# Keys and values of an 8-head attention made in an earlier stage, kept in DRAM and fetched batch by batch

## The reference

```python
x = x + tanh(g_xattn[0]) * cosine_similarity(layernorm(x), c)       # L0 attention
x = x + tanh(g_ffn[0])   * top2_of_8_linear_experts(layernorm(x))   # L0 ffn
x = x + tanh(g_xattn[1]) * film_s4d_block(layernorm(x), c)          # L1: top-32 attention, FiLM, S4D
x = x + tanh(g_ffn[1])   * adapter_of_least_loss(layernorm(x))      # L1 ffn
x = x + tanh(g_xattn[2]) * attention_16_heads(layernorm(x), c)      # L2 attention
x = x + tanh(g_ffn[2])   * fp8_linear(layernorm(x))                 # L2 ffn
x = x + tanh(g_xattn[3]) * attention_8_heads(layernorm(x), c)       # L3 attention
x = x + tanh(g_ffn[3])   * top2_of_8_gelu_experts(layernorm(x))     # L3 ffn
```

```python
q = (x @ Wq).reshape(B, Nq, 8, 64)
k = (context @ Wk).reshape(B, 128, 8, 64)
v = (context @ Wv).reshape(B, 128, 8, 64)
attn = softmax(einsum('bihd,bjhd->bhij', q, k) * SCALE)
out = einsum('bhij,bjhd->bihd', attn, v).reshape(B, Nq, 512) @ Wo + bo
```

## Time and profile before

| | |
|---|---|
| device time, median of 3 runs | 1424.72 us (1424.49 to 1426.15) |
| the profiled execution | 1425.62 us, its span 1423.8 us |
| mean granted TensorE clock | 0.868 |
| busy share of the span | PE 83%, DVE 70%, ACT 48%, POOL 39% |
| top-32 attention with its start and end | from about 211 to 479.6 us |
| convolution | 479.6 to about 494 us |
| 8-head attention with the fp8 layer | from about 895 to 1155 us; its first scores start at 921.7 us |

### The profile page before, as it was taken

How to read it: one execution, slowest core, us unless ns; L and a number is a source line. 1 busy time by engine, 2 the same in 40 slices (tenths; PEclk the granted TensorE clock), 3 DMA queues, 4 the chain that set the end, 5 groups by cost and what they waited for, 6 DMA issues and landing times. The chain is left out here.

```text
span 1423.8 us, 30767 instructions
## 1 busy us (share of the span) xinstructions
PE 1177.9 (83%) x10551; PEld 807.0 (57%) x10551; DVE 995.2 (70%) x3895; ACT 689.7 (48%) x2022; POOL 548.2 (39%) x770
## 2 busy tenths in 40 slices
PE   4768664767766858996899998699999989999998
PEld 3534322434444535663777777266667667776776
DVE  6767568999999269976577877677776644444433
ACT  3344245677775244432345454366666643333343
POOL 4576665677764246534122321334433310000000
PEclk8788785776675779998799999699999999898989
DMA  6400104000001311101000000000000000000000
GB/s 171 99 0 1 46 12 131 16 24 27 27 23 45 115 64 42 38 23 34 3 3 3 3 4 3 1 1 1 1 2 1 2 0 1 15 0 15 0 16 15
DMA packets 61249, 36.62 MB, mean 26 GB/s; under 512 B 19477, under 2 KB 58992, under 8 KB 61106
## 3 DMA queue, kind: packets, MB, share of 16 engines
q1 hardware_dynamic: 59802, 34.48, 8.5%
q10 hardware_dynamic: 1304, 0.33, 0.1%
HBM read 25.21 MB, written 6.42 MB: 22 GB/s over the span
## 5 line engine op out<-in xcount | busy, mean ns | idle before, releaser
L3032 DVE SCALAR_TENSOR_TENSOR k_X<-ps,m_gt,k_X 128x128 f32 (+1 forms) x256 | 72.1, 344 | 120.9 <-PE ps L2916 120.9
L2955 ACT ACTIVATE m_hid<-ps,k_b 128x512 f32<-128x512 f32 x128 | 81.9, 684 | 133.0 <-PE ps L2916 127.6
L2916 PEld LDWEIGHTS ps<-k_w,m_hid 128*128 128x128 f32 x1024 | 123.1, 192 | 26.8 <-issue 19.6
L2905 PE MATMUL ps<-m_xnT,k_w 128*128 128x512 f32 x256 | 128.1, 631 | 1.3 <-PEq L72 1.3
L2916 PE MATMUL ps<-k_w,m_hid 128*128 128x128 f32 x1024 | 123.4, 275 | 0.0
L2576 POOL TENSOR_TENSOR l_p<-l_p,l_rsum 128x512 f32<-128x512 f32 x64 | 65.3, 1041 | 138.0 <-DVE l_rsum L2854 138.0
L2284 DVE TENSOR_REDUCE g_peak<-ps 128x8 f32<-128x1024 f32 x64 | 75.4, 1220 | 43.0 <-PE ps L1973 43.0
L2708 ACT ACTIVATE l_p<-ps,l_shift 128x128 f32<-128x128 f32 x256 | 91.6, 390 | 21.5 <-DVE l_shift L2795 20.3
L1587 DVE MATCH_REPLACE8 v_left<-c_top,v_left 128x128 f32<-128x128 f32 x384 | 100.8, 275 | 0.0
L711 PE MATMUL ps<-f_expT,f_xeT 128*128 128x512 f32 x128 | 77.3, 739 | 27.2 <-DVE k_X L1089 27.2
L2179 ACT ACTIVATE g_pT<-ps 128x1024 f32<-128x1024 f32 x64 | 62.0, 1021 | 71.6 <-PE ps L1989 71.6
(11 more groups left out here) (538 smaller groups left out, 3145.8 us busy)
## 6 DMA issues: line engine op xcount, KB each, us to landing
v_toep<-kpad SPq DMA_DIRECT2D x4, 1024.0 KB, 9.2
fo_dram<-c_fo SPq DMA_DIRECT2D x32, 128.0 KB, 1.7
g_v<-fo_dram SPq DMA_DIRECT2D x8, 512.0 KB, 3.7
d_mine<-d_wad SPq DMA_DIRECT2D x32, 96.5 KB, 1.9
k_X<-in_x SPq DMA_DIRECT2D x8, 256.0 KB, 3.6
v_late<-kpad SPq DMA_DIRECT2D x2, 1024.0 KB, 8.1
out<-k_X SPq DMA_DIRECT2D x8, 256.0 KB, 2.4
f_cx<-in_ctx SPq DMA_DIRECT2D x4, 384.0 KB, 5.4
```

Of the source, the lines that this page charges most:

```text
L2905: pe.matmul(ps[:, 4 * u + q, :], k.w1_3[:, e, 128 * q:128 * q + 128], xnT[:, u], start=True, stop=True).then_inc(s["hid_ps"].sem, 1)
L2916: m = pe.matmul(ps[:, 4 * u + 2 + e % 2, j * S:j * S + S], hid[:, u, q, j * S:j * S + S], k.w2_3[:, e, q, :], start=q == 0, stop=q == 1)
L2955: act.activation(hid[:, u, q, :], ps[:, 4 * u + q, :], ACT.Gelu, bias=k.b1_3[:, 2 * e + q:2 * e + q + 1]).then_inc(s["hid"].sem, 1)
L3032: dve.scalar_tensor_tensor(out=xj[u][j], in0=ps[:, 4 * u + 2 + e % 2, j * S:j * S + S], scalar=gt[:, u, j, e:e + 1], in1=xj[u][j], op0=ALU ...
```

## The change

The keys and values of all 32 batches are made in `film_in`: for batch i a new TensorE block `values_keys(i)` makes, for each of four 128-column slices, the values (context as weights, `wv3` moving) and the keys (`wk3` as weights, context moving) into columns 128 to 383 of banks 0 to 3, beside the scores. ScalarE's new `spilled(i)` copies 128x1024 out into `kv`, and SyncE's `keep_kv(i)` writes it to `kv_dram`. The block of a pair's first batch stands in front of the next pair's first scores, that of the second batch in front of its second scores; `spilled` stands behind each `scored`. To make room in SBUF, `EARLY` goes from 4 to 3, so that three chunks are loaded in `convolve`. In `fp8_attention8` the matmuls of keys (L2621, L2700) and values (L2655) go, with their copies (L2718, L2758, L2814) and the waits `k_done` and `v_done`; SyncE fetches 512 KB a batch into one of three buffers.

```diff
-EARLY = CHUNKS // 2
+EARLY = 3
...
+            def keep_kv(i):
+                sp.wait_ge(kv_done, i + 1)
+                sp.dma_start(k.kv_dram[:, i, :], kv[:, i % 2].rearrange("p h c -> p (h c)")).then_inc(k.kv_out[i % 2], 16)
+
+            for i in range(4):
+                keep_kv(i)
             for i in range(B):
...
                 sp.wait_ge(fo_done, i + 1)
                 sp.dma_start(k.fo_dram[:, i:i + 1, :].rearrange("s b c -> s (b c)"),
                              fo[:, i % 2, 256:512]).then_inc(k.fo_out[i % 2], 16)
+                if i % 2 and i + 4 < B:
+                    keep_kv(i + 3)
+                    keep_kv(i + 4)
...
+            def values_keys(i):
+
+                pe.wait_ge(sc_done, min(i + 2, B))
+                if i:
+                    pe.wait_ge(kv_done, i)
+                c = slice(S * i, S * i + S)
+                for h in range(4):
+                    q = slice(128 * h, 128 * h + 128)
+                    pe.matmul(ps[:, h, 128:256], k.cT[:, c], k.wv3[:, q], start=True, stop=True)
+                    m = pe.matmul(ps[:, h, 256:384], k.wk3[:, q], k.cT[:, c], start=True, stop=True)
+                m.then_inc(kv_ps, 1)
...
+                if pair(p):
+                    values_keys(2 * p)
                 if pair(p + 1):
                     scores(2 * (p + 1))
...
+                    pe.wait_ge(kv_done, B)
                     pe.transpose(ps[0:1, 0, 0:128], wmax[:], k.ident[:]).then_inc(wmax_T, 1)
...
+                if pair(p):
+                    values_keys(2 * p + 1)
                 if pair(p + 1):
                     scores(2 * (p + 1) + 1)
...
+            def spilled(i):
+                act.wait_ge(kv_ps, i + 1)
+                if i >= 2:
+                    act.wait_ge(k.kv_out[i % 2], 16 * (i // 2))
+                act.activation(kv[:, i % 2], ps[:, 0:4, 128:384], ACT.Identity).then_inc(kv_done, 1)
...
                 if pair(p + 1):
                     scored(2 * (p + 1), p)
                 if pair(p):
+                    spilled(2 * p)
+                if pair(p):
                     whole(2 * p + 1)
                 if pair(p + 1):
                     scored(2 * (p + 1) + 1, p)
+                if pair(p):
+                    spilled(2 * p + 1)
...
+                sp.wait_ge(k.kv_out[a], 16 * B // 2)
...
+        @block.sync
+        def _(sp):
+            for i in range(B):
+                if i >= 3:
+                    sp.wait_ge(av_ps, i - 2)
+                sp.dma_start(kv[:, i % 3].rearrange("p h c -> p (h c)"), k.kv_dram[:, i, :]).then_inc(kv_in[i % 3], 16)
...
                     pe.wait_ge(q_done, 4 * (i // G + 1))
+                    pe.wait_ge(kv_in[i % 3], 16 * (i // 3 + 1))
...
-                    pe.matmul(ps[:, 6, :], k.wk3[:, 128 * b:128 * b + 128], k.cT[:, W * g:W * g + W], start=True,
-                              stop=True).then_inc(k_ps, 1)
...
-                    pe.matmul(ps[:, 7, :], k.cT[:, S * i:S * i + S], k.wv3[:], start=True, stop=True).then_inc(v_ps, 1)
...
-                    pe.wait_ge(v_done, n + 1)
...
-                    act.activation(kT[:, g % 2, b, :], ps[:, 6, :], ACT.Identity).then_inc(k_done, 1)
...
-                dve.tensor_copy(v[:, i % 2], ps[:, 7, :]).then_inc(v_done, 1)
```

More of the change, by code:

```diff
@@ L1187, in stage_film @@
         k.fo_out = [once(f"fo_out{i}") for i in range(2)]
+        k.kv_out = [once(f"kv_out{i}") for i in range(2)]
         k.sc = ctx.enter_context(nc.sbuf_tensor("v_sc", [128, CH, 128], F32))
@@ L1227, in film_in @@
         fo = tmp("fo", [128, 2, 512])
+        kv = tmp("kv", [128, 2, 4, 256])
         once = ctx.enter_context(OneTime(nc, "c_"))
@@ L1247, in film_in @@
         flip_ps, flipped = once("flip_ps"), once("flipped")
+        kv_ps, kv_done = once("kv_ps"), once("kv_done")
         block = ctx.enter_context(nc.Block())
@@ L2520, in fp8_attention8 @@
                               "xnT_done"))
-        k_ps, k_done, q_ps, q_done, v_ps, v_done = (
-            once(n) for n in ("k_ps", "k_done", "q_ps", "q_done", "v_ps", "v_done"))
+        q_ps, q_done = once("q_ps"), once("q_done")
+        kv_in = [once(f"kv_in{i}") for i in range(3)]
         sc_ps, top_done, shift_done, p_done, rsum_done, share_done, pT_ps, pT_done, av_ps, oT_done, out_ps, x_done = (
@@ L2533, in due @@
             return g if (n + lead) % G == 0 and 0 <= g < GROUPS else None
-        def keys(n):
-            return {-15: 0, -14: 1, -11: 2, -10: 3}.get(n)
         def bank(g, b):
@@ L2626, in _ @@
                     pe.wait_ge(oT_done, i + 1)
-                    pe.wait_ge(v_done, min(i + 2, B))
+                    if i:
+                        pe.wait_ge(x_done, i)
                     pe.wait_ge(x8_done, begun(n - 1, 11))
@@ L2647, in _ @@
                             m.then_inc(pT_ps, 1)
[L2648 to L2654, removed]
-                    pe.matmul(ps[:, 7, :], k.cT[:, S * i:S * i + S], k.wv3[:], start=True, stop=True).then_inc(v_ps, 1)
                 g, b = item(n)
                 if g is not None:
-                    pe.wait_ge(k_done, 4 * g + b + 1)
                     pe.wait_ge(xnT_done, g + 1)
+                    if g:
+                        if 4 * g + b > 4:
+                            pe.wait_ge(q_done, 4 * g + b)
+                        pe.wait_ge(xqT_done, begun(n - 1, 12))
                     pe.matmul(ps[:, bank(g, b), :], k.wq3[:, 128 * b:128 * b + 128], xnT[:, g % 2, :], start=True,
@@ L2667, in _ @@
                             h = 2 * b + a
-                            m = pe.matmul(ps[DH * a:DH * a + DH, 4, 128 * b:128 * b + 128], v[:, n % 2, DH * h:DH * h + DH],
+                            m = pe.matmul(ps[DH * a:DH * a + DH, 4, 128 * b:128 * b + 128], kv[:, n % 3, b, DH * a:DH * a + DH],
                                           pT[:, n % 2, 4 * a + b, :], start=True, stop=True)
@@ L2697, in _ @@
                     m.then_inc(o8_ps, 1)
-                b = keys(n)
-                if b is not None:
-                    pe.matmul(ps[:, b, :], k.wk3[:, 128 * b:128 * b + 128], k.cT[:, 0:W], start=True,
-                              stop=True).then_inc(k_ps, 1)
         @block.scalar
@@ L2712, in _ @@
             for n in range(FIRST, LAST):
-                g, b = item(n)
-                if g:
-                    act.wait_ge(k_ps, 4 * g + b + 1)
-                    if g >= 2 and b == 0:
-                        act.wait_ge(sc_ps, G * (g - 1))
-                    act.activation(kT[:, g % 2, b, :], ps[:, 6, :], ACT.Identity).then_inc(k_done, 1)
                 if 0 <= n + 1 < B:
@@ L2754, in _ @@
                                    scale=scale[:]).then_inc(q8_done, 1)
-                b = keys(n - 1)
-                if b is not None:
-                    act.wait_ge(k_ps, b + 1)
-                    act.activation(kT[:, 0, b, :], ps[:, b, :], ACT.Identity).then_inc(k_done, 1)
         @block.vector
```

22 lines of the change are left out of this document (6 added, 16 removed).

## The result

The changed kernel takes 1472.1 us (median of 4 runs, 1467.8 to 1475.4) against 1424.6 for the kernel before on the same chip: a ratio of 1.0323, 95% interval 1.0299 to 1.0347. It is 47.5 us slower. The forecast was 18.5 us slower with a range that ended at 1478. The direction was right, the size was 29 us short of the measured one. The profiled execution took 1474.4 us for a span of 1472.6.

The account below looks back on a forecast made before the run. It took VectorE to pace the top-32 stage and a chain through several engines, not TensorE's matmuls, to pace the 8-head attention. +20 +0.5 -2 = +18.5 us gave 1443 against the median 1424.7, range 1412 to 1478.

Parts of the forecast that it names:

- -2 (-10 + 8): 8-head attention: 10 us gained by shorter batches, 8 us lost to clock falls; between -10 and +19.
- 6.66 to 6.29: 8-head attention: the shortest of four repeating batch spacings falls to 6.29 us; 11 batches, 4.1 us.
- 7.28 to about 6.6: 8-head attention: the 7.28 us batch spacing falls to about 6.6 us, an estimate; 5 batches, 3.3 us.
- four falls of the clock: 8-head attention: idle gaps halve TensorE's clock four times, 2.1 us each, 8 us taken in all.
- A batch can't fall below 6.29 us: 8-head attention: the chain from scores through exponentials and evacuation to the value product, untouched by the change, takes 6.29 us.
- the term +20: Top-32 stage: 16.6 us a pair, 1.55 over VectorE's 15.07, in 13 of 16 pairs: 20 us; bounds 0 and 65.
- (1) c_aT for L1424: Top-32 stage: the first product block delays the product that ScalarE's c_aT waits for; mean 0.7 us a pair.
- (2) second scores: Top-32 stage: second block waits for the first evacuation, second scores behind it; 0.8 us full clock, 2.9 half, 2.7 taken.
- (3) c_fo: Top-32 stage: ScalarE's c_fo comes behind the later film products; 0.4 us a pair.
- 13 pairs: Top-32 stage: the early scores' lead covers some pairs, so 13 of 16 pay the excess over VectorE's pace.
- Rival (C): Clock stays low through most of a top-32 pair and falls in attention's gaps: up to 1509 us; chance 0.20.
- +0.5: Convolution: the third late chunk lands at 491.0 us, with the last chunk starting at 491.43 today; 0.5 us, between 0 and 2.

Follow-up runs that it names:

- kernels 1: The changed kernel with the 8-head attention of the kernel before, which makes its own keys and values: 1478.6 us.
- kernel 15: The kernel before with three early Toeplitz chunks in place of four, nothing else: 1426.4 us, ratio 1.0003.
- kernel 12: The changed kernel with 8-head attention reordered: queries, output product, transposes, scores of batch n + 2, then product with the values: 1448.6 us.
- kernel 7: The changed kernel with unused TensorE products ahead of the second product block in pairs 2 to 13 of the top-32 stage: 1436.8 us.
- kernel 5: The changed kernel with only the first two batches' keys and values written to DRAM and fetched in turn: 1474.0 us.
- kernel 9: The changed kernel with the top-32 stage reordered: first product block behind the next pair's head sums, second ahead of the film products: 1425.8 us.
- 16: The kernel before with scores of batch n + 2 issued ahead of batch n's product with the values, VectorE's maximum moved too: 1459.6 us.
- 17: The kernel before with early scores in an order made like that of kernel 12, keys and values still made in the attention: 1452.6 us.

## Why the forecast was right in direction and short in size

**8-head attention.** Forecast -2 (-10 + 8), measured -6.5. The chain came out batch by batch behind the opening: "6.66 to 6.29" is 6.22 to 6.28, "7.28 to about 6.6" is 6.61, and 7.5 and 7.8 stayed. L2700's waits, forecast near 2 us, are 1.01, 1.21, 1.70 and 2.17 us in turn:

```profile
1003.10 1.09 PE L2700 MATMUL ps<-l_pT,l_kv 128*64 128x128 f32 x16 [1.71 <-ACT l_pT L2754]
...
1009.91 1.09 PE L2700 MATMUL ps<-l_pT,l_kv 128*64 128x128 f32 x16 [1.22 <-ACT l_pT L2754]
...
1016.18 1.09 PE L2700 MATMUL ps<-l_pT,l_kv 128*64 128x128 f32 x16 [1.01 <-ACT l_pT L2754]
...
1023.69 1.09 PE L2700 MATMUL ps<-l_pT,l_kv 128*64 128x128 f32 x16 [2.17 <-ACT l_pT L2754]
```

65 us of matmuls left and 6.5 us came back. That -2 and -6.5 lie close is in part luck, since three of its parts missed. From the third batch's scores to the last the stretch is 8.4 us shorter although a fall of the clock cost 0.8 in it, so the batches gave some 9.2 us where 7.4 were forecast. The opening gave nothing where 3 us were forecast: the second batch's scores follow the first's 1.8 us sooner, but the third's come 10.25 instead of 8.30 us behind, because TensorE idles 3.67 us for GpSimd (1.19 before) and then runs at half clock. And four falls of the clock were forecast at 2.1 us each. There were four, at 985.6, 1081.2, 1173.3 and 1187.0, but the one in mid-stage (1081.2) cost nothing: it made the scores and the output product 1.5 us longer, the next wait of L2700 shrank from 1.70 to 0.63 us, and the batch took 7.73 us like the others of its kind (7.76). That of 1173.3 made its batch 7.04 us long instead of 6.28. The gain itself depends on the trace it is taken against: kernels 1 and 15 hold the old attention too and take 2.5 us more for it than the trace before, with one fall in the opening.

By the rule of the Trainium skill on weight loads ("Perfetto Trace Analysis", section "Identifying the Most-Contended Engine") that the forecast held beside its own sum the gain would be nothing, by the busy matmuls 65 us; 6.5 lies close to the rule. "A batch can't fall below 6.29 us" holds only for this order; kernel 12 shows 5.50. The chain runs through the queues of three engines, and a queue's order can be changed.

**Top-32 stage.** This is the step that failed: the term +20 measured +53.6 (+51.6 by the moment at which the convolution begins). Per pair:

| ScalarE, us a pair | forecast | measured |
|---|---|---|
| busy | 12.8 | 12.7 |
| (1) c_aT for L1424 | 0.7 | 0.86 |
| (2) second scores | 2.7 | 2.9 |
| (3) c_fo | 0.4 | 0.4 |
| head sums (L1414) | none | 1.45 |
| flipped x (L1469) | none | 0.4 |
| sum | 16.6 | 18.8 |

The mechanism and the three waits that I named came out to within 0.2 us each. Two waits were left out of the sum. ScalarE's wait for the head sums at the pair's start was there before as well, 26.5 us in this stretch, but as slack behind VectorE. With the slack gone, and the head sums behind the second block, the second scores and a half clock, it became a part of the loop. In kernel 7 it shrinks to 4.5 us. The pair is 18.8 - 15.07 = 3.73 us over VectorE's pace, not 1.55. By the starts of the first-round maxima the first three pairs are as long as before, the next twelve are 48.4 us longer together (4.0 each), and 5.2 us come behind the start of the last pair's maxima, which the forecast did not have. It had 13 pairs: their size and not their number was wrong. Behind it stands one decision: I took the low clock for wait (2) alone and let the rest run at full clock, because "once behind, TensorE has 12 us without a break". The row from 399 to 406 us shows that of such unbroken work the first 7 us still run at 0.55. Rival (C)'s 20.1 us a pair is the nearer figure to 18.8, but its words, "the clock stays low through most of the pair", don't hold either: a mean of 0.77 is the low level for 46% of the time, less than before the change (0.70, 60%). What changed is not how long the clock is low but what runs meanwhile: work that ScalarE waits for. Its second half, clock under 0.9 in the attention, did not come (0.98 from 977 to 1187 us).

**Convolution.** Forecast +0.5, measured +2.4 there; kernel 15 puts the chunk itself at +1.6 within the stretch and at +0.4 (-1.7 to +2.4) over all; the other 0.8 us stay open. The three transfers land 10.5 us after their issue in the median (9.5 in kernel 15), the two before landed after 8.1, a slowing that the forecast left out; and the three issues take 7.97 us on SyncE's queue where two took 3.29, so the third goes out later than I had added up.

**What cost nothing.** The writes (kernel 5) and the fetches (512 KB land in 3.6 us, and L2655 idles 0.6 us in all, for the queries and not for a fetch).

The rule on banks that the forecast quoted (the Trainium skill, "Perfetto Trace Analysis", section "Optimizing Tensor Performance") asks for independent groups in different banks. The runs agree in part: kernel 9 keeps the shared banks and loses 5.1 us of the stage instead of 53.6. What mattered was that no engine had to wait for the shared bank while others waited for it.

## What to carry to other kernels

When an engine seems to have room (ScalarE with 4 us of 15 here), list all its waits in the loop, those that are slack today too, since they become cost as soon as the slack is used. Work that two engines hand to each other through shared banks belongs where neither has anything due, directly behind other work of TensorE: the same products and copies cost 53.6 us of the stage in one place and 5.1 in another. Before work is moved off the busiest engine, look for the chain that runs through its queue: removing 65 us of matmuls gave 6.5 us, and reordering what was left gave 24. The two belong together: with the matmuls still there, the reorderings that I tried (16, 17) made the kernel slower.

## What the runs showed of the hardware

TensorE did the kernel faster by doing more: unused products in 12 pairs took 35 us off, because the granted clock of that stretch went from 0.77 to 0.97. In the 8-head attention gaps of 1.0 to 1.7 us in each batch left the clock at 1.00; one of 2.17 us ahead of L2700 at 1079.90 was followed by a fall at 1081.2 us (four windows of 1 us, the clock third from the end), which made the scores and the output product 0.9 + 0.6 = 1.5 us longer:

```profile
1080.00:1081.00 1.00, 1.00 (x18) 0.83 (x19) 0.00 (x0) 1.00 (x8) 0.00 (x0) 1.00 0.00 0
1081.00:1082.00 1.00, 1.00 (x10) 0.86 (x12) 0.72 (x3) 0.24 (x2) 0.44 (x1) 0.58 0.00 0
1082.00:1083.00 1.00, 1.00 (x14) 1.00 (x12) 0.70 (x2) 0.00 (x0) 1.00 (x2) 0.50 0.96 152
1083.00:1084.00 1.00, 1.00 (x7) 0.78 (x6) 0.58 (x1) 0.00 (x0) 1.00 (x2) 0.50 0.89 365
```

Equal gaps ahead of 1023.69 and 1051.79 left it at 1.00, and shorter ones, 1.88 and 1.87 us ahead of 1172.14 and 1185.46, were followed by a fall, so the length of a gap alone does not tell whether the clock falls.
